# Audio tower, two layers with a mixture of experts: the first MLP up block ahead of the router's transposes on TensorE

## What is computed

```python
h = tok(x)                      # pairs of steps, softmax-weighted: 64 x 128 tokens
h = h + rwkv_attention(ln(h))   # layer 0
h = h + gelu(ln(h) @ up.T + b) @ down          # layer 0, the tower MLP: 192 -> 768 -> 192
h = h + attention_12_heads(ln(h))              # layer 1
h = h + experts(ln(h))          # layer 1: router over 8 experts, best 2, gelu MLP 192 -> 768 -> 192
```

## Time and profile before

| | us |
|---|---|
| median of the 3 timed runs | 1794.03 |
| lowest and highest of them | 1791.66 and 1804.02 |
| time of the profiled execution | 1808.08 |
| its span | 1806.3 |
| PE busy in it | 1576.6 (87%) |
| DVE busy | 1369.8 (76%) |
| ACT busy | 1192.0 (66%) |

### The profile page before, as it was taken

One profiled execution on the slowest core, in us unless ns is written; L12 is line 12 of the kernel. 1 busy time (PEld: TensorE's weight loads), 2 busy tenths in 40 slices (PEclk: granted clock), 3 DMA queues, 4 the chain that ended last, 5 costly groups with the idle time before them and its releaser, 6 DMA issues.

```text
span 1806.3 us, 33908 instructions
## 1 busy us (share of the span) xinstructions
PE 1576.6 (87%) x10985; PEld 1269.9 (70%) x10985; DVE 1369.8 (76%) x2810; ACT 1192.0 (66%) x3269; POOL 739.9 (41%) x743
## 2 busy tenths in 40 slices
PE   3578999999999999999999887763999999999976
PEld 2255677677677677677677666543999999999876
DVE  4675788778788788778778743334899989999986
ACT  1245787877887787778778767543666666666643
POOL 0111142332332333333233232203577777777775
PEclk6798899989999899989989978656999999999988
DMA  4000010110110111011010000244677776677662
GB/s 118 26 27 17 20 51 28 43 51 26 41 50 31 36 50 38 30 50 44 24 50 30 22 34 25 99 148 146 168 169 167 172 160 159 160 166 171 159 152 64
DMA packets 121870, 145.41 MB, mean 81 GB/s; under 512 B 21074, under 2 KB 100419, under 8 KB 121795
## 3 DMA queue, kind: packets, MB, share of 16 engines
q1 hardware_dynamic: 92432, 113.00, 20.8%
q0 software_dynamic: 26592, 29.92, 8.9%
q10 hardware_dynamic: 2770, 1.56, 0.3%
HBM read 92.74 MB, written 46.77 MB: 77 GB/s over the span
## 4 chain that ended last, share of the span: by engine, by line
PE 74%; DVE 9%; ACT 8%; issue 4%; SPq 2%; POOL 1%; DMA 1%; POOLq 0%; ACTq 0%; DVEq 0%
PE ps L934 12%; PE ps L947 9%; PE ps L716 7%; PE ps L791 5%; PE ps L702 5%; PE ps L949 4%; PE ps L807 4%; PE ps L597 3%; PE ps L708 3%; PE ps L556 3%; PE ps L737 3%; PE ps L820 2%; PE ps L749 2%; ACT probs L1091 2%; PE ps L603 2%
## 5 line engine op out<-in xcount | busy, mean ns | idle before, releaser
L1330 POOL DMA_INDIRECT out<-ey,etoken x142 | 253.9, 1788 | 143.6 <-DVE ey L1847 48.4
L1091 ACT ACTIVATE probs<-ps,nmax 128x128 f32<-128x128 f32 x768 | 272.2, 397 | 24.2 <-DVE nmax L1570 24.1
L947 PE MATMUL ps<-w_hl,h_hi 128*128 128x384 f32 x852 | 252.3, 366 | 12.3 <-DVE ey L1847 12.3
L1203 ACT ACTIVATE h_full<-ps,eb 128x512 f32<-128x512 f32 (+1 forms) x234 | 158.4, 677 | 154.0 <-PE ps L934 153.8
L1570 DVE TENSOR_REDUCE nmax<-ps 128x6 f32<-128x768 f32 x128 | 121.5, 953 | 134.1 <-PE ps L791 133.0
L949 PE MATMUL ps<-w_hl,h_lo 128*128 128x192 f32 x852 | 215.4, 253 | 0.0
L1091 ACT ACTIVATION_READ_ACCUMULATOR probs<-ps,nmax 128x1 f32 x768 | 182.1, 237 | 0.0
L1320 POOL TENSOR_TENSOR w_lo<-w_raw,w_hi 128x1536 fp32r<-128x1536 f32 x39 | 156.5, 4013 | 39.4 <-ACT w_hi L1183 39.4
L947 PEld LDWEIGHTS ps<-w_hl,h_hi 128*128 128x128 f32 x852 | 162.8, 191 | 13.7 <-issue 13.2
L949 PEld LDWEIGHTS ps<-w_hl,h_lo 128*128 128x128 f32 x852 | 165.3, 194 | 0.0
L1807 DVE TENSOR_TENSOR h_lo<-h_full,h_hi 128x512 fp32r<-128x512 f32 (+1 forms) x234 | 148.0, 686 | 16.7 <-ACT h_hi L1204 16.3
(11 more groups left out here) (303 smaller groups left out, 3915.7 us busy)
## 6 DMA issues: line engine op xcount, KB each, us to landing
w_raw<-in_L_ffn_w SPq DMA_DIRECT2D x39, 576.0 KB, 4.8
ex<-expert_rows_in SPq DMA_DIRECT2D x32, 528.0 KB, 5.4
w_raw<-in_L_ffn_w SPq DMA_DIRECT2D x39, 384.0 KB, 5.3
w_raw<-in_L_ffn_w SPq DMA_DIRECT2D x78, 192.0 KB, 5.7
xt<-in_x SPq DMA_DIRECT2D x16, 768.0 KB, 4.5
expert_rows_in<-xt SPq DMA_DIRECT2D x17, 528.0 KB, 7.0
hA_kept<-hA SPq DMA_DIRECT2D x16, 384.0 KB
out<-resC SPq DMA_DIRECT2D x16, 384.0 KB, 2.6
```

The costliest lines, as they stand in the source:

```text
L947: nc.tensor.matmul(ps[:, 4 + s, 0:2 * C], h_hi[b][:, m, q], w2_hl[b][:, m, :], start=(m == 0), stop=False)
L1091: last = nc.scalar.activation(probs[:, t % 2, HJ * c + j, :], ps[:, 4 + j, c * P:(c + 1) * P], ACT.Exp, bias=nmax[:, t, j, c:c + 1], accum ...
L1203: nc.scalar.activation(h_full[:, m, 0:n], ps[:, m % 4, 0:n], ACT.Gelu, bias=eb1[u][:, m:m + 1])
L1330: nc.gpsimd.indirect_dma_start(total, bass.IndirectOffsetOnAxis(ap=etoken[u][:, s:s + 1], axis=0), ey[b][:, s, :], None, bounds_check=NB * ...
```

## The change

In PE's round, and there alone, block 0 of the tower MLP's up-projection is issued ahead of the router's transposes.

```diff
                 if gb is not None: b_transposes(gb)
                 if gn is not None: a_scores(gn)
+                if gb is not None: b_mlp_up(gb, 0)
                 if gr is not None: r_transposes(gr, gc)
-                if gb is not None: b_mlp_up(gb, 0)
                 if gb is not None: b_mlp_up(gb, 1)
                 if gr is not None: r_logits(gr)
```

## The result

The changed kernel took 1838.85 us (median of 4 runs, 1820.92 to 1843.74) against 1799.03 us (median of 4, 1791.66 to 1804.89) for the kernel before beside it. The ratio is 1.0167, with a 95% interval of 1.0117 to 1.0218; the quotient of the two medians is larger, 1.0221. The changed kernel is slower by both, and 1838.85 us lies above the 1824 at which the prediction's range ended.

A forecast was written before the change was run, and what follows sets the result against it. PE's queue was taken to bound the kernel through its software-pipelined round. Wait 10.0 us plus seams 2.0, clock 0, gave +12.0 on the 1794.0 median: 1806 us, 0.7% slower, range 1788 to 1824.

The forecast's parts named there:

- The wait: PE ahead of block 0: waiting for DVE's hTB_lo adds 0.66 us in ten rounds, 0.85 in four; 10.0 us.
- Who only follows: ACT and DVE behind PE: first GELU 1.4 us later, hidden before block 2; later idle times give nothing back.
- rival c: Later waits in the round swallow the cost: about 1795 us; chance 0.05.
- rival d: Block 0 fills PE's idle 1.21 us ahead of the transposes, saving 10.9 us: 1783 us; chance 0.03.
- The seams: PE's switches between matmul kinds around block 0 and the transposes: 0.14 us a round, 2.0 us in all (1.3 to 2.7).
- The clock: PE's granted clock over the twelve rounds: taken as 0, with ends of 26.5 us less and 36.4 us more.
- rival (b): PE's longer pause brings more clock falls, or 69.04 us rounds become the rule: 1824 (half) to 1842 us; chance 0.20.
- rival (a): Most rounds keep granted clock 1.00, as four of twelve already do, repaying the wait: fully 1780 us; chance 0.15.
- The place of the falls: PE at 1.2 GHz behind the router logits and the small score matmuls, else 2.4 GHz; both places stay.
- The weight load: PE's load for block 0 stays behind the semaphore wait; pulled out, it would save some 0.1 us a round, 1.4 in all.

The follow-up runs named there:

- fill_after: Changed kernel plus seven extra matmuls of constants in PE's pause ahead of block 0; 1830.3 us, ratio 1.0146 to the kernel before.
- wait_only: Kernel before, its order kept, with the router's transposes also waiting for hTB_lo; 1826.2 us, ratio 1.0130; on the fifth chip 1918.6 us, 1.0409.
- three fillers: Extra matmuls of constants in three idle places of PE's round; added to the kernel before: 1882.8 us (1.0086) and 1880.5 us (1.0047).
- early_low: Changed kernel with hTB_lo's subtraction ahead of the q and k statistics on DVE; 1791.5 us, ratio 0.9929 to the kernel before.
- before_again: Kernel before, unchanged, run once more for a second trace on the fourth chip; 1880.5 us, one run.

## Why the prediction was wrong, point by point

- **The wait.** The mechanism was right, and so was its size. Block 0 waits for hTB_lo, 1.88 us (1.8 to 1.9 foretold), the transposes stand behind it, and a round at 1.00 is 64.53 us (fill_after), +0.75 against 0.66 + 0.14 = 0.80 foretold. Over the twelve rounds that makes 9.0 us, of the 12 us for all 14.
- **Who only follows.** Right for PE. Block 2 has no idle time, block 4 has 0.56 us, and nothing swallows the cost (rival c) nor is the gap filled (rival d). hTC is later: ACT stands idle 3.21 us ahead of it, where it was 1.25. Against the end of the scores it starts 1.95 us later, where 1.46 followed from the prediction's times, and the first GELU 2.2 us later instead of 1.4. The transposes and block 1 ran partly at the low clock, and the GELU waits 0.30 us for block 1, which I hadn't counted.
- **The seams.** Within the bounds: 0.75 less 0.66 is 0.09, the lower end of the 0.09 to 0.19.
- **The clock.** Here the prediction failed: "No row shows a preference, so I take 0." The step took the clock as a term of zero mean with wide ends. The twelve rounds are 26.7 us longer, and 9.0 of it is the wait, so 17.7 us is the clock, twice the wait; PE's time at 1.2 GHz in them went from 68 to 106 us. At the 0.4 us for each us at the low clock that the rounds of 63.78 and 65.14 us give (1.36 us for 3.4), that is an estimate of 15 us. Before, a round cost on average 791.75 / 12 - 63.78 = 2.2 us over its length at 1.00; in the changed kernel it is 818.44 / 12 - 64.53 = 3.7 us. It was rival (b), with a chance of 0.20, that came: half of its 36.4 us gave 1824 and all of it 1842, and the median was 1838.85. The median moved by 39.8 us, some 11 of them for the wait (14 rounds); the traces account for less, since the traced execution of the kernel before (1808.1 us) was slower than all its timed ones.
- **Two readings of the clock rows.** Three of the twelve rounds were at 1.00, not four as rival (a) has it. And the round of 69.04 us has two falls, not one: PE ran at 1.2 GHz from 563.5 to 566.9 too, behind the logits, so "else at 2.4 GHz" is wrong. Neither changes the sum.
- **The place of the falls.** The text said that they stand behind the logits and the score matmuls and stay there. They do, and in the changed kernel a new one stands right behind the pause, in 10 of the twelve rounds. In the round shown above it is the stretch that begins within the transposes:

```profile
495.04:498.45 3.41, 3.41 (x15) 2.45 (x13) 3.33 (x3) 2.19 (x2) 0.32 (x2) 0.51 0.00 0
```

That a pause of 1.9 us, then three dense matmuls and eight transposes, would let it fall was named under (b). The round at 163.46, which the prediction read for its seams, already had that pause in the kernel before. It holds an MLP group and no router group, so the change doesn't touch it. A little further on in it than the rows go, the matmuls take 0.63 us instead of 0.39:

```profile
163.46 0.50 PE L702 MATMUL ps<-hTB,up_hi 128*128 128x512 f32 x1 [1.93 <-DVE hTB_lo L1557]
...
164.02 0.53 PE L702 MATMUL ps<-hTB,up_lo 128*128 128x512 f32 x1
164.35 0.63 PE L702 MATMUL ps<-hTB,up_hi 128*128 128x512 f32 x1
```

and the busy time of that stretch has the granted clock at 0.51:

```profile
164.05:167.46 3.41, 3.36 (x11) 1.70 (x9) 3.38 (x4) 0.01 (x1) 0.97 (x2) 0.51 0.00 0
```

So a row with a preference was at hand, with no transposes behind the pause at all. In the 20 traces of this case the pause in that round is 1.92 to 1.93 us in 14, and the clock falls behind it in 12 of these; in the six in which it is 0.29 to 0.72 us, the clock falls behind it in none. wait_only shows the same for the rounds in question: the pause is enough, without the new order, and not in every round.
- **The weight load.** The Trainium skill ("TensorE: Matmul & The Clock Gate", section "Part 2: What happens when you issue a matmul") has weight loads pulled ahead of matmuls in flight. In the changed kernel the load for block 0 starts at 493.83 with its matmul, after 2.17 us without a load, so it stayed behind the semaphore wait, as the row said.

What stays open: why the clock falls behind the pause in nearly every round of one execution and hardly any of another, what makes up the loss on the second chip, why three fillers don't help the kernel before on the chips with the outside wait, and whether early b_low with block 0 first is a gain at all beyond the first chip.

## What to carry to other kernels

An idle gap is only worth filling with work whose own input is there before the gap ends: look up when the last producer of the moved work's input ends (here 493.20) beside the end of the gap (492.46), and count everything that stands behind the moved wait. Where PE is the bound and its granted clock wavers between 1.00 and 0.90 round by round, a longer pause is not paid once: in the first two traces each 0.75 us of wait came with about 1.5 us more that went to the low clock (17.7 us in twelve rounds). Before such a term is put at 0, look in the trace for a place that already has a pause of the new length, and read the clock behind it. A change of under a per cent on such a kernel should be run on more than one chip before it is kept.

## What the runs showed of the hardware that was not expected

The granted clock falls into a pattern that repeats with the round: in the kernel before a trio of 63.8, 65.1 and 69.0 us, in early_low 64.9 us nearly each time, in the changed kernel a pattern of six rounds from 66.1 to 71.2 us. A change of 0.75 us in the round's length goes with another pattern.

The same program differs by chip by more than the change is worth. On four of five chips ACT's tanh in the tower waited about 5 us a round for something outside the core, and PE behind it. From the trace of before_again, the view of that line:

```profile
L1045 ACT ACTIVATE tanh_r<-ps x16: 810/810/811, 39.9 to 1046.8; 128x768 f32<-128x768 f32 x16
...
  remote: 56.6, 11
  PE ps L605: 32.0, 5
```

The ratios on the fourth and fifth chip have the lower times of the kernel before under them, while its only trace there is of an execution of 1880.5 us. Only the comparisons between the other kernels of these chips are free of that. What the wait is for, no run here shows.
